# Graph network, first stage: mesh product in three fp32r products, attribute scatters split 14 and 156

## The reference, cut to what matters

```python
for l in range(3):                       # _L0_gnn_ref
    neigh = segment_sum(h[src], dst) * inv_deg
    h = h @ Ws_self[l] + neigh @ Ws_neigh[l] + bs[l]
    if l != 2: h = relu(h)
x = layernorm(x + h)
e = mlp(edge_attr_4, emb)                # _L1_gnn_ref
e_in = concatenate([e, mesh_nfeat[src], x[dst]])
e_new = mlp(e_in, edge) + e              # e_in @ edge_W0: three blocks of 512 rows
agg = segment_sum(e_new, dst)
n_new = mlp(concatenate([x, agg]), node) + x
return layernorm(x + n_new)
```

## Time and profile before

| | |
|---|---|
| three executions | 2256.23, 2258.77, 2259.15 us, median 2258.77 |
| profiled execution | 2256.75 us |
| its span | 2255.0 us |
| PE matmul, weight load busy | 97%, 83% of the span |
| DVE, ACT, POOL busy | 67%, 54%, 54% |
| POOL attribute scatters (L145) | 170 in 224.4 us, 1320 ns each |

### The profile page before, as it was taken

The page is one execution under the profiler, slowest core; times in us unless marked ns, Lnnn a source line. Parts: engine busy times, 40 slices in busy tenths (PEclk is TensorE's granted clock), DMA queues, the critical chain, the costliest instruction groups (busy, mean ns, idle before and its releaser), DMA issues. The chain is left out here.

```text
span 2255.0 us, 44895 instructions
## 1 busy us (share of the span) xinstructions
PE 2190.3 (97%) x13039; PEld 1881.9 (83%) x13040; DVE 1502.7 (67%) x3372; ACT 1218.0 (54%) x2244; POOL 1206.8 (54%) x1721
## 2 busy tenths in 40 slices
PE   7999989999999999999999999999999999999898
PEld 4367888888789989899898998989989989889776
DVE  8425975344756777767767667766776676767666
ACT  2221114333256676677666767667667667667421
POOL 0775028885535555565555555555555555555223
PEclk9999999999999999999999999999999999999899
DMA  6421001112363333323332333333323332333131
GB/s 203 127 56 41 0 6 40 8 40 54 114 210 88 64 62 63 62 60 65 60 65 61 65 60 65 63 63 60 65 60 60 65 65 61 60 65 65 27 92 44
DMA packets 81814, 149.81 MB, mean 66 GB/s; under 512 B 20523, under 2 KB 20989, under 8 KB 81754
## 3 DMA queue, kind: packets, MB, share of 16 engines
q0 software_dynamic: 47248, 93.38, 21.5%
q1 hardware_dynamic: 34505, 55.67, 7.8%
HBM read 128.90 MB, written 19.71 MB: 66 GB/s over the span
## 5 line engine op out<-in xcount | busy, mean ns | idle before, releaser
L1667 ACT ACTIVATE b_bank<-c_bias 128x512 f32<-128x512 f32 x528 | 316.4, 599 | 15.1 <-PE b_bank L1779 10.0
L145 POOL DMA_INDIRECT s_attrs<-k_attrs,k_row_i x170 | 224.4, 1320 | 168.0 <-POOLq L2233 117.2
L1600 DVE CUSTOM_DVE_ANT_0 b_bank<-b_bank,c_p,k_floor 128x512 f32<-128x512 f32 x176 | 132.5, 753 | 255.5 <-PE b_bank L1801 254.6
L1445 POOL DMA_INDIRECT c_from_src<-s_dst_table,c_at_nodes x173 | 278.5, 1610 | 32.2 <-issue 32.2
L1856 PE MATMUL b_bank<-k_m_hi,c_pt_hi 128*128 128x512 f32 x704 | 293.8, 417 | 0.0
L1432 POOL DMA_INDIRECT c_from_src<-s_mesh_table,c_at_nodes x176 | 202.3, 1149 | 152.3 <-POOL c_at_nodes L1428 142.5
L1857 PE MATMUL b_bank<-k_m_lo,c_pt_hi 128*128 128x512 f32 x704 | 277.9, 395 | 0.0
L1451 POOL TENSOR_TENSOR c_dev<-c_var,k_half 128x1 f32<-128x1 f32 x176 | 99.3, 564 | 327.5 <-DVE c_var L1582 327.5
L1858 PE MATMUL b_bank<-k_m_hi,c_pt_lo 128*128 128x512 f32 x704 | 273.9, 389 | 0.0
L1738 ACT ACTIVATE c_h<-c_from_src 128x512 f32<-128x512 f32 x176 | 111.3, 632 | 263.4 <-DVE c_from_src L1621 263.4
L1799 PE MATMUL b_bank<-c_m_hi,c_ht_hi 128*128 128x384 f32 x704 | 222.5, 316 | 6.3 <-DVE c_ht_lo L1587 6.0
(11 more groups left out here) (352 smaller groups left out, 5859.9 us busy)
## 6 DMA issues: line engine op xcount, KB each, us to landing
c_from_src<-s_mesh_table,c_at_nodes POOLq DMA_INDIRECT x176
c_from_src<-s_dst_table,c_at_nodes POOLq DMA_INDIRECT x173, 4.7
s_attrs<-k_attrs,k_row_i POOLq DMA_INDIRECT x170
a_mesh<-in_L_gnn_mesh_nfeat_dram SPq DMA_DIRECT2D x10, 224.0 KB
k_h<-in_x_dram SPq DMA_DIRECT2D x10, 224.0 KB
s_mesh_table<-a_mesh_out SPq DMA_DIRECT2D x10, 224.0 KB
b_x<-in_x_dram SPq DMA_DIRECT2D x10, 224.0 KB
s_node_own<-b_out SPq DMA_DIRECT2D x10, 224.0 KB
```

Source lines behind the costliest of these rows:

```text
L145: return pool.indirect_dma_start(scratch["attrs"], bass.IndirectOffsetOnAxis(ap=k["row_i"][0:EP, c:c + 1], axis=0), k["attrs"][0:EP, A4 * ...
L1445: pool.indirect_dma_start(from_src[u][:], None, scratch["dst_head" if head else "dst_table"], bass.IndirectOffsetOnAxis(ap=at_nodes[u][:, ...
L1600: dve.tensor_tensor_reduce(var1_bank[:], var1_bank[:], p[u % 2][:], 1.0 / D, k["floor"][:, 0:1], ALU.mult, ALU.add, var[u][:, 0:1]).then_i ...
L1667: act.activation(bank[:], bias[:, m, :], ACT.Copy).then_inc(bank_set, 1)
```

## The change

The mesh product is computed as the first layer's is. `w0b_hi` and `w0b_lo` are its weights' high and low part; ACT makes the first after the second vector product's row copy, DVE the second, in the place of `w0b`. ACT's copy of the turned block becomes the high part (`mesh_t` is now fp32r), and DVE makes a low part `mesh_lo` from the bank and it. `w0b_hi` lies where `w0a` was, and `mesh_lo` where `wnb` was. PE multiplies block n and turns block n + 2 behind it, and all loops over mesh blocks are written out. ACT, and no longer SP, issues the loads of blocks 2 to 9, each behind its copy of the block two before. `w_hi` and `w_lo` move between mesh blocks. SP's load of `bias0` goes ahead of the mesh stores. ATTR_EARLY is 14 in place of 24, so 14 attribute columns are scattered ahead of POOL's gates and 156 among the layers, 140 of them at once.

```diff
-ATTR_EARLY, ATTR_LATE, ATTR_PAIR = 24, 16, 4
+ATTR_EARLY, ATTR_LATE, ATTR_PAIR = 14, 16, 4
...
+W0A_AT, WNB_AT, W0B_AT = (FOLD_AT + n * KC * D * 4 for n in (6, 7, 8))
...
-    mesh_t = [fd(f"mesh_t{i}", [P, KC, P]) for i in range(2)]
+    mesh_t = [fd(f"mesh_t{i}", [P, KC, P], F32R) for i in range(2)]
...
+    w0b_hi = Region(nc, W0A_AT, SBUF_END)("a_w0b_hi", [P, KC, D], F32R)
+    w0b_lo = Region(nc, W0B_AT, SBUF_END)("a_w0b_lo", [P, KC, D], F32R)
+    late_low = Region(nc, WNB_AT, SBUF_END)
+    mesh_lo = [late_low(f"a_mesh_lo{i}", [P, KC, P], F32R) for i in range(2)]
...
-        with sp.Fori(0, NB // 2 - 1) as i:
-            for u in range(2):
-                sp.wait_ge(mesh_turned, 2 * i + u + 1)
-                move_rows(sp, mesh[u][:], node_rows(t["L1_gnn_mesh_nfeat"], 2 * i + 2 + u), mesh_in[u])
-            for u in range(2):
-                sp.wait_ge(mesh_ok, 2 * i + u + 1)
-                move_rows(sp, node_rows(scratch["mesh_table"], 2 * i + u), mesh_out[u][:], mesh_stored[u])
...
+        sp.dma_start(bias0[:], rows(t["L0_gnn_bs"][0]).broadcast_to([P, D])).then_inc(bias_in, 16)
+        for n in range(NB):
             sp.wait_ge(mesh_ok, n + 1)
-            move_rows(sp, node_rows(scratch["mesh_table"], n), mesh_out[u][:], mesh_stored[u])
-
-        sp.dma_start(bias0[:], rows(t["L0_gnn_bs"][0]).broadcast_to([P, D])).then_inc(bias_in, 16)
+            move_rows(sp, node_rows(scratch["mesh_table"], n), mesh_out[n % 2][:], mesh_stored[n % 2])
...
         for c in range(ATTR_EARLY):
-            scatter_attr(pool, scratch, k, c).then_inc(attr_scattered[c // BACKLOG % 2], 16)
+            scatter_attr(pool, scratch, k, c).then_inc(attr_scattered[0], 16)
         open_gates(pool, 1)
...
+        def mesh_low(n, u, fixed):
+            dve.wait_ge(mesh_t_ok, n + 1)
+            if not fixed:
+                dve.wait_ge(mesh_mm, n - 1)
+            dve.tensor_tensor(mesh_lo[u][:, :, 0:NPB], spread(bank[4 + u]), mesh_t[u][:, :, 0:NPB].bitcast(F32),
+                              ALU.subtract).then_inc(mesh_lo_ok, 1)
+
+        dve.wait_ge(w0b_hi_ok, 1)
+        dve.tensor_tensor(w0b_lo[:], w0b[:], w0b_hi[:].bitcast(F32), ALU.subtract).then_inc(w0b_ok, 1)
...
+        for n in range(NB):
+            mesh_copy(n, n % 2, n < 2)
+            if n + 2 < NB:
+                mesh_low(n + 2, n % 2, False)
+            if n in (2, 4):
+                i = n // 2 - 1
+                dve.wait_ge(w_hi_ok, i + 1)
+                dve.tensor_tensor(w_lo[i][:], w[i][:], w_hi[i][:].bitcast(F32), ALU.subtract).then_inc(w_lo_ok, 1)
...
+            if r == 1:
+                act.activation(w0b_hi[:], w0b[:], ACT.Copy).then_inc(w0b_hi_ok, 1)
...
+        def mesh_load(n):
+            act.wait_ge(mesh_turned, n - 1)
+            move_rows(act, mesh[n % 2][:], node_rows(t["L1_gnn_mesh_nfeat"], n), mesh_in[n % 2])
+
         for u in range(2):
             mesh_copy(u, u, True)
+            mesh_load(2 + u)
         act.wait_ge(next_in, NB * MOVED + 4 * 16)
         for i in range(2):
             act.activation(w_hi[i][:], w[i][:], ACT.Copy).then_inc(w_hi_ok, 1)
+            mesh_copy(2 + i, i, False)
+            mesh_load(4 + i)
...
         def multiply(n, u, fixed):
-            pe.wait_ge(mesh_t_ok, n + 1)
-            if not fixed:
+            pe.wait_ge(mesh_lo_ok, n + 1)
+            if fixed:
+                pe.wait_ge(w0b_ok, 1)
+            else:
                 pe.wait_ge(mesh_ok, n - 1)
-            for c in range(KC):
-                last = pe.matmul(bank[6 + u][0:NPB, :], mesh_t[u][:, c, 0:NPB], w0b[:, c, :], start=(c == 0), stop=(c == KC - 1))
-            last.then_inc(mesh_mm, 1)
+            left = (lambda c: mesh_t[u][:, c, 0:NPB], lambda c: mesh_lo[u][:, c, 0:NPB])
+            product(pe, bank[6 + u][0:NPB, :], left, (lambda c: w0b_hi[:, c, :], lambda c: w0b_lo[:, c, :]),
+                    range(KC)).then_inc(mesh_mm, 1)
 
         for u in range(2):
             turn(u, u, True)
-        for u in range(2):
-            multiply(u, u, True)
-        with pe.Fori(1, NB // 2) as i:
-            for u in range(2):
-                turn(2 * i + u, u, False)
-            for u in range(2):
-                multiply(2 * i + u, u, False)
+        for n in range(NB):
+            multiply(n, n % 2, n < 2)
+            if n + 2 < NB:
+                turn(n + 2, n % 2, False)
```

More of the change, by code:

```diff
@@ L245, in phase_a @@
     scattered = [sem(f"scattered{i}") for i in range(2)]
-    attr_scattered = [sem(f"attr_scattered{i}") for i in range(2)]
+    attr_scattered = [sem("attr_scattered0")]
     pairs_in, pairs_read, pairs_turned = sem("pairs_in"), sem("pairs_read"), sem("pairs_turned")
@@ L575, in mesh_copy @@
             dve.tensor_copy(mesh_out[u][:], bank[6 + u][0:NPB, :]).then_inc(mesh_ok, 1)
-        for u in range(2):
[L578 to L582, removed]
-            for u in range(2):
-                mesh_copy(2 * i + u, u, False)
+        def mesh_low(n, u, fixed):
[6 more added lines that the diff above has]
+        dve.tensor_tensor(w0b_lo[:], w0b[:], w0b_hi[:].bitcast(F32), ALU.subtract).then_inc(w0b_ok, 1)
+        for u in range(2):
+            mesh_low(u, u, True)
+        for n in range(NB):
[6 more added lines that the diff above has]
+                dve.tensor_tensor(w_lo[i][:], w[i][:], w_hi[i][:].bitcast(F32), ALU.subtract).then_inc(w_lo_ok, 1)
         def low(n):
@@ L689, in _ @@
             copy_h(n)
-        with act.Fori(1, NB // 2) as i:
-            for u in range(2):
-                mesh_copy(2 * i + u, u, False)
+        for n in range(4, NB):
+            mesh_copy(n, n % 2, False)
+            if n + 2 < NB:
+                mesh_load(n + 2)
         def high(n):
@@ L783, in turn @@
             if not fixed:
-                pe.wait_ge(mesh_t_ok, n - 1)
+                pe.wait_ge(mesh_lo_ok, n - 1)
             for c in range(KC):
```

5 lines of the change are left out of this document (3 added, 2 removed).

## The result

| | before | changed |
|---|---|---|
| median of the runs (us) | 2258.96 (4 runs, 2256.23 to 2259.49) | 2246.18 (4 runs, 2245.02 to 2247.47) |
| profiled execution: time, span (us) | 2256.75, 2255.0 | 2246.75, 2245.0 |

The ratio is 0.9945, with a 95% interval of 0.9933 to 0.9957: 12.8 us less by the medians, 10.0 between the two profiled executions. Forecast were 2243 us and 15 to 16 less.

The account below looks back on a forecast made before the run. PE, busy 97% of the span, was taken as the bound. Terms of -7.7, -7.3 and 0 sum to -15.0 us, from 2256.75 to 2241.7; forecast 2243 us with the median's offset, range 2238 to 2250.

Parts of the forecast that it names:

- the creeping: Start of counting stage, from its fifth tile: engines advance slowly until POOL's last early scatter ends at 207.35; seventh tile at 207.66.
- term 1: Mesh stage on PE: twelve fp32r products a block for four f32; ends at 127.8, not 135.50: -7.7 us.
- both things that I costed at nothing: Mesh stage: ACT's added loads and copies and DVE's low tiles hold PE up by nothing, between 0 and 3 us.
- Term 2: Counting stage: ten scatters fewer ahead of the gates shorten the creeping, -7.3 us, between 0 and 8.3 besides 0.4 of clock.
- with 14 the last ends at 192.4: POOL ahead of the gates: at 1.493 us a scatter, 14 end at 192.4 where 24 ended at 207.35.
- the creeping lasts until POOL's last scatter: Counting stage: if creeping needs POOL at its scatters, it can last only from 190.5 to 192.4.
- Term 3: Layers: ten more scatters take POOL 16.1 of 19.73 us idle before the first deviation; slack 3.6, cost 0.
- A: Counting: creeping stays, a first pass through new loop code, whatever POOL does; term 2 is 0: 2249 us; chance 0.15.
- B: Mesh stage: waits of 0.3 us a block on the ACT and DVE chain take 3 us of term 1: 2246; chance 0.08.
- C: Layers: ten scatters cost over 19.7 us, POOL 5.4 us late to the first deviation: 2247 us; chance 0.06.
- D: Mesh stage: loads issued by ACT land late, the whole is slower: 2259.7 us, 2262 with the median's 2; chance 0.03.
- E: Mesh stage: the products are not made as three fp32r ones; given no chance of its own.

Follow-up runs that it names:

- the later comparisons: Kernel before and changed kernel, both unchanged, run again beside the experiments: before 2252.36 us; changed 2244.91 us (ratio 0.9967), a third time 2244.82 us (0.9969).
- products alone: Changed kernel with ATTR_EARLY back at 24 in place of 14: 2247.05 us, ratio 0.9977 to the kernel before.
- the run with four: Changed kernel with ATTR_EARLY = 4, so 166 attribute columns among the layers: 2256.54 us, ratio 1.0021 to the kernel before.
- the run with loads on SyncE: Changed kernel with mesh loads of blocks 2 to 9 back on SP, each ahead of a store in one queue: 2251.76 us, ratio 0.9999.
- 104 increments more: Changed kernel with 104 idle semaphore increments on ScalarE: 2242.4 us (ratio 0.9961); with the three subtractions also in four parts: 2244.79 us (0.9968).

## Why the prediction was right, and where it was not

The forecast's direction and bracket held: 2246.18 in 2238 to 2250, 3.2 us above the number given. Part of this is luck. Half of the 15.0 us of the sum rested on the creeping, and the measurement that was forecast happened to have it in the kernel before. In the later comparisons the change gives 7.3 to 7.5 us, near term 1 alone.

**Term 1 was right to 0.01 us.** Forecast 7.7, measured 41.26 - 33.55 = 7.71, and the same stage length to 0.01 in all profiles that keep its loads and turns. The product's price taken from the first layer's rows (0.233) was the right one; the estimate from the Trainium skill ("FP8 and Floating Point Precision", TensorE Precision Notes), 2.61 us for a block's products, would have been 1.9 us too short over ten. One reading in the prediction is off: 39.94 / 5 - 6.97 is 1.02, and the 1.27 for a pair of turns and its wait comes out as (39.94 - 5 x 6.97) / 4; the sum doesn't use it. "No wait of PE" held as well, and so did the reasons: both things that I costed at nothing are what keeps it at nothing, since loads on SP cost 8.4 us and turns in pairs 6.3. ACT's two issues took 1.09 us in the first load and 0.77 in the others, and copy 2 began at 100.56, near the 99.9 of my chain. The stage began 0.7 us later than before; the first turn stood anywhere between 95.1 and 98.0 in the twelve profiles of the experiments, with no bearing of the edits on it that I can see, so I give that to no part of the change.

**Term 2: the link to POOL's last scatter held in the two first profiles; its size was 7.3 and measured 4.6; and the creeping is not in every execution of the kernel.** The step "with 14 the last ends at 192.4" failed: it took POOL's pace of before for granted, and left out what DVE's new long subtraction, and the two moved ones, do to POOL. The last scatter ended at 195.9, and the seventh tile came at 196.85 instead of by 194, short of the 199 that was to refute the term. The step "the creeping lasts until POOL's last scatter" was right in that profile. But products alone (scatters to 211, nothing crept in steps) and the kernel before itself, which did not creep in its second profile and ran below 2255.3 us on all three chips, show that it takes more than POOL's scatters; what that is was not found. My account of the creeping rested on one profile. Clear of it, the counting stage of before and changed kernel differs by 10.71 - 9.97 = 0.7 us. What no term had is that the products alone would lengthen it: they bring counting forward, on to the scatters, beside which DVE's small one-hot takes up to 0.58 us and not 0.24. With the products and 24 columns the stretch takes 11.86 us, with 14 it takes 9.97, so behind the products the ten scatters are worth 1.9 (2.2 by the medians of the two on one chip, 2247.05 and 2244.82); in the kernel before they are worth 0.9 (10.71 and 9.81).

**Term 3 was right, with less room than forecast.** Slack 3.6 forecast, 1.89 measured in the first profile and 3.45 in the second; ten scatters took 16.9 us more in the first pair of profiles and 17.3 in the second, against 16.1, and from POOL's first scatter to the deviation it was 0.9 and 0.4 us less than before, where the prediction had it unchanged. That POOL's lateness is paid in full from the edge on is shown by the run with four.

**What no term had: +2.2 us in the edge stage**, which the change doesn't touch. With the missing 2.7 of term 2 and the 0.7 of the later start, less some 0.5 among the layers and behind them (at the start of the layers PE's granted clock was 1.2 GHz for 3.4 us and not for 6.8), it makes the 5.0 us between 15.0 and the 10.0 of the two profiles. It goes with the instructions that stand ahead of ScalarE's edge loop: the unrolled copies and loads added some, without the loads (the run with loads on SyncE) the 2 us were not lost, and with 104 increments more they were not lost either. That the position of the loop's code is the reason was only argued, and the forecasts by counting instructions missed twice and came true once.

**The rivals.** A, the creeping stays: it stayed, but ended with POOL. Its mechanism, a first pass through new code, would have cost the same whatever POOL did, and the same program shows none of it in its second profile; yet its sum, 7.7 us less, is the one nearest to the later comparisons. B, 0.3 us a block: no wait (its 2246 is reckoned from 2243, while A and C start from the profiled execution, so it stands 1.3 us too high beside them). C, POOL late to the deviation: not with ten, but it is how four columns end. D, late loads: not with ACT; its price is that of the loads on SP, 8.4 us, by another way (the queue's order, not the landing). E, other products: the rows show the first layer's form, L73 to L75, twelve a block.

## What to carry to other kernels

Cost a product form by rows of the same shape and type, and ask for each load which queue it stands in and behind what. When a term rests on a stall that no row explains, profile the kernel before a second time first, on another chip if there is one: 7.1 us of the counting stage were not there the second time. When one stage is brought forward, ask which work of another engine it now runs beside. And a long vector instruction added beside POOL's scatters is a cost to them, even on an engine with time to spare; cut into parts it costs them a quarter of that or less (0.48 us and not 1.97), but four instructions for one move what follows in the engine's program, and the edge stage stayed at 1468.4 us with them even behind the 104 increments.

## What the runs showed of the hardware

- A scatter that POOL begins while DVE subtracts 128x2048 out of two SBUF tiles ends 1.07 us after that instruction does, so a 1.19 us scatter took up to 3.16 in the first profile (3.27 in the third). In four parts, at most 1.67. By the Trainium skill ("SBUF — State Buffer", Who interferes with whom) the port pair that VectorE shares with GpSimd is an exclusive lock, and VectorE's second SBUF input comes through its read interface. The trace agrees for the scatter. It shows no hold the other way: the subtraction at 108.24 began while a scatter of 1.19 us was running, and took its 2.28 us.
- The same program, without any change, took 2256 to 2259 us in its first measurement and 2249 to 2255 beside the experiments, on three chips; which chip the first ran on is not on record. In the profiles the two differ by 7.1 us in the counting of the first 16 tiles, where the queues of PE, DVE, POOL and SP moved in steps of some 0.74 us while POOL scattered. Neither the two first profiles nor the twelve others, none of which has it, tell why, and whether it hangs on the chip or on the execution is open too.
- While POOL scatters, DVE's one-hot of 128x128 took 0.28 and 0.58 us by turns and that of 128x1280 0.74 and 0.54; clear of the scatters they took 0.24 and 0.54.
- One step of an engine's loop takes longer or shorter with what stands ahead of the loop in its program, and nearly the same in each pass: ScalarE's third activation behind its jump started 0.52 or 0.60 us after the second, VectorE's first wait 0.09 or 0.19 after the step before it. By the Trainium skill ("Runtime: NRT & Kernel Launch", Instruction fetch mechanics) a taken branch whose target is out of the fetched window stalls; that this is such a case no run here shows, and ScalarE's late activation starts 2.9 us behind the jump.
